# Dense inputs moved from the last chunk of z to the last chunk of turned sums in a DLRM tower, and an order laid out anew

## What is computed

```
e   = stack(tbl_f[ids[:, f]] for f in range(40))      # 2048 x 40 x 64
z_p = sum over d, c of e_i[d] * W_p[d, c] * e_j[c]    # 780 pairs
h   = concat([z, dense_ctx])                          # 780 + 16 = 796 inputs
h   = relu(h @ W_top1 + b_top1)                       # 796 -> 512
h   = relu(h @ W_top2 + b_top2)                       # 512 -> 256
y   = h @ W_top3                                      # 256 -> 1
```

## Time and profile before

| | us |
|---|---|
| median of 3 runs | 1236.45 (1236.43 to 1236.52) |
| the profiled execution | 1235.92 |
| its span, first to last instruction | 1234.1 |
| PE busy | 1216.8 (99%) |
| DVE busy | 1004.4 (81%) |
| ACT busy | 954.5 (77%) |
| POOL busy | 781.1 (63%) |

### The profile page before, as it was taken

The page is one execution under the profiler, slowest core; times in us unless marked ns, Lnnn a source line. Parts: engine busy times, 40 slices in busy tenths (PEclk is TensorE's granted clock), DMA queues, the critical chain, the costliest instruction groups (busy, mean ns, idle before and its releaser), DMA issues.

```text
span 1234.1 us, 23139 instructions
## 1 busy us (share of the span) xinstructions
PE 1216.8 (99%) x5912; PEld 445.5 (36%) x5912; DVE 1004.4 (81%) x916; ACT 954.5 (77%) x7377; POOL 781.1 (63%) x1038
## 2 busy tenths in 40 slices
PE   7999999999999999999999999999999999999999
PEld 3333333333333333333333333333333333333333
DVE  7898999998787788898767868889787876788850
ACT  2174878998383889999688899999778899999841
POOL 8888883686655577777656666778766566423320
DMA  7332222222222222222222222222222222111100
GB/s 200 110 86 66 67 75 58 70 70 65 64 64 60 50 76 64 65 75 63 70 58 59 68 57 66 67 74 65 61 71 65 62 59 61 54 49 57 43 10 1
DMA packets 68477, 81.00 MB, mean 66 GB/s; under 512 B 15308, under 2 KB 46028, under 8 KB 68216
## 3 DMA queue, kind: packets, MB, share of 16 engines
q1 hardware_dynamic: 48752, 59.42, 16.1%
q0 software_dynamic: 19456, 19.96, 9.0%
q10 hardware_dynamic: 136, 0.14, 0.0%
HBM read 79.45 MB, written 0.01 MB: 64 GB/s over the span
## 4 chain that ended last, share of the span: by engine, by line
PE 95%; DVE 3%; issue 1%; ACT 1%; DMA 0%; SPq 0%; DVEq 0%
PE u_ps L940 35%; PE u_ps L936 23%; PE z_ps L957 19%; PE turn_ps L988 7%; PE turn_ps L908 3%; PE turn_ps L901 2%; PE turn_ps L998 2%; PE u_ps L988 2%; DVE acts L1051 1%; DVE fprod L1088 1%; PE u_ps L998 1%; PE turn_ps L974 1%; DVE rprod_A L1075 0%; DMA rows<-in_first_ids 0%; PE turn_ps L1007 0%
## 5 line engine op out<-in xcount | busy, mean ns | idle before, releaser
L1145 ACT ACTIVATE rprod_A<-rprod_A 128x64 f32<-128x64 f32 x3616 | 866.3, 242 | 105.2 <-DVE rprod_A L1075 102.7
L845 POOL DMA_INDIRECT rows<-in_tbl,ids_all x608 | 575.3, 946 | 274.1 <-issue 112.6
L1145 ACT ACTIVATION_READ_ACCUMULATOR rprod_A<-rprod_A 128x1 f32 x3616 | 680.3, 188 | 0.0
L1088 DVE TENSOR_TENSOR fprod<-u_ps,x 128x1024 f32<-128x1024 f32 x480 | 567.4, 1219 | 50.6 <-PE u_ps L940 50.0
L940 PE MATMUL u_ps<-x,wf_ring 64*128 64x512 f32 x1920 | 490.1, 607 | 3.6 <-ACT x L1132 1.8
L1075 DVE TENSOR_TENSOR rprod_A<-u_ps,rows 128x1024 f32<-128x1024 f32 x226 | 274.9, 1222 | 131.5 <-PE u_ps L936 131.5
L936 PE MATMUL u_ps<-wr_ring,x 64*128 64x512 f32 x1280 | 347.5, 612 | 0.7 <-DVE rprod_A L1075 0.5
L940 PEld LDWEIGHTS u_ps<-x,wf_ring 64*128 64x128 f32 x1920 | 175.1, 186 | 252.9 <-issue 186.7
L957 PE MATMUL z_ps<-fprod,ones 128*32 128x512 f32 x1920 | 251.9, 598 | 0.0
L865 POOL TENSOR_TENSOR rprod_P<-rprod_P 128x512 f32<-128x512 f32 (+4 forms) x245 | 148.5, 606 | 131.3 <-DVE rprod_P L1075 115.4
L936 PEld LDWEIGHTS u_ps<-wr_ring,x 64*128 64x128 f32 x1280 | 116.7, 186 | 171.2 <-issue 93.7
(11 more groups left out here) (37 smaller groups left out, 193.2 us busy)
## 6 DMA issues: line engine op xcount, KB each, us to landing
wf_ring<-in_w_standing SPq DMA_DIRECT2D x240, 128.0 KB
wr_ring<-in_w_moving SPq DMA_DIRECT2D x80, 256.0 KB
rows<-in_tbl,ids_all POOLq DMA_INDIRECT x608
mlp_sb<-in_mlp SPq DMA_DIRECT2D x1, 2308.0 KB, 9.6
mlp_sb<-in_tbl SPq DMA_DIRECT2D x6, 224.0 KB
rows<-in_first_ids SPq DMA_DIRECT2D x4, 256.0 KB, 5.8
rprod_P<-in_first_ids SPq DMA_DIRECT2D x4, 256.0 KB, 8.8
mlp_sb<-in_tbl SPq DMA_DIRECT2D x2, 280.0 KB
```

The costliest lines, as they stand in the source:

```text
L845: nc.gpsimd.indirect_dma_start(rows[:, v % ROW_SLOTS, s, par * DIM:(par + 1) * DIM], None, tables[f], bass.IndirectOffsetOnAxis(ap=ids_all ...
L1088: nc.vector.tensor_tensor(fprod[:, f % FPROD_SLOTS], u_ps[:, bank:bank + 2, :], other, ALU.mult).then_inc(prods_done, 1)
L1145: op = nc.scalar.activation(of[:, j, :], of[:, j, :], ACT.Copy, accum_out=sums_at(u, j, 1))
```

## The change

DENSE_CHUNK and DENSE_ROW become the last chunk of turned sums and row 64 there (they were chunk 3 of z, row 96). With this `z_strips` gives four strips for the last chunk of z as well, `move_z` copies 128 rows of it in place of 96, layer 1 reads 128 rows of chunk 3 in place of 112 and 80 rows of chunk 6 in place of 64, and the dense DMA goes to z_sb's slot for chunk 6. That slot is one for all blocks, while the four chunks of z go round six slots. `lay_mlp` lays out W_top1 to match, on the host. Of the plan, seven constants are changed; the order of all steps is computed from them.

```diff
-DENSE_CHUNK, DENSE_ROW = (ZF - 1, 96) if Z_LAST <= 48 else (ZK - 1, R_PAIRS % P)
-assert Z_LAST <= 48 or 0 < DENSE_ROW <= P - DENSE
+DENSE_CHUNK, DENSE_ROW = (ZK - 1, R_PAIRS % P) if 0 < R_PAIRS % P <= 64 else (ZF - 1, 96)
+assert DENSE_CHUNK >= ZF or Z_LAST <= 48
...
-T_HOT, T_BUILD, T_TABLE, T_TABLES = 0.423, 0.35, 6.0, 1.6
-
-LEAD, LEAST, ROWS_LEAD = 4, 1, 4
-
-STALL, GAP = 0.05, -0.3
-
-MLP_GAP, MLP_PACE = 6, 14
+T_HOT, T_BUILD, T_TABLE, T_TABLES = 0.423, 0.535, 8.5, 1.6
+
+LEAD, LEAST, ROWS_LEAD = 8, 1, 5
+
+STALL, GAP = 0.05, 0.2
+
+MLP_GAP, MLP_PACE = 2, 12
```

## The result

The change makes the kernel faster by 2.3%: 1208.57 us (1208.33 to 1208.88, 4 runs) against 1236.44 us, a ratio of 0.9775 with a 95% interval of 0.9758 to 0.9792. That is 27.9 us where 22.6 were forecast. A second group of runs gave 0.9778 [0.9761, 0.9794].

What follows compares the result with a forecast made beforehand. The prediction took PE (busy 99%) as the bound, with DVE setting the pace in block 0 from 120 to 275 us. It summed -19.7 (strips) - 4 (start) + 1.1 (ROWS_LEAD) = -22.6, giving 1213.8 us, range 1207 to 1221.5.

Steps and rivals of the forecast that it cites:

- The group of sums: Chunk 3's 24 groups on PE: four strips cut each from 2.70 to 1.86 us, 20.4 on PE, -19.7 at the end.
- The estimate from the speedups of 3.07 and 2.38: Chunk 3's groups on PE: 2.09 us each, 14.6 saved in all; as a rival 1218.9 us, 3%.
- 18 x 0.85 come through: Last groups of blocks 1 to 3, where DVE waits for PE: 15.3 us of the strips' saving reaches the end.
- fillers: LEAD 8 and MLP pacing move duos and MLP steps to other stalls: 0, bounds -4 to +4 us.
- The start term (-4): Start of block 0: quad 2's moving units near 109 us instead of 115.31, closing DVE idle time; bounds 0 and -6.3.
- the price of 1.1: Block 0: ROWS_LEAD 5 moves one unit's sum from POOL to DVE, +1.1 us; extremes +8 and -5.
- the term of 4.4: DVE's six gaps after block 0's last groups: saving cut to the gap, 0.56 + 0.47 + 4 x 0.85 us.
- a bound of 1.6 for heights in layer 1: Layer 1's heights of 80 and 128 rows put at 0; bound 32 instructions by 49 ns, either way.
- Block 0 didn't eat its share: Rival: the order gives nothing and saturated DVE in block 0 turns PE's saving into waiting; -15.3 alone, 1221.2 us, 20%.
- the filler wasn't used up: Rival: MLP_GAP 2 spends MLP steps early in blocks 1 to 3, up to 57 us lost; half gives 1242, 5%.
- the change did what it said: Denies the rival that four-strip groups still wait for their products and nothing is gained: 1236 us, 2%.
- the rival of a better gain: Start's hole closes fully (-6.3), fewer V sums in block 0 (-4), all 20.4 of the strips: 1205.8 us, 8%.

## Why the prediction held, and where it was short

**The group of sums.** Right in size and in count: 1.86 us forecast, 1.85 measured, in 23 of 24 groups. The estimate from the speedups of 3.07 and 2.38 in TensorE: Matmul & The Clock Gate of the Trainium skill ("Measured speedup vs the span model") would have given 2.09, and the trace decides against it here. The 3.07 stands there for four row tiles, and these strips are column tiles, so the two speedups weren't of one kind. The step that failed in a small way is "18 x 0.85 come through": the very last group waits for its products (0.05 gained), so it is 17.

**Blocks 1 to 3.** -16.6 us to the last unit, where 17 groups give 14.5. The other 2.1 are left for the order, whose fillers the prediction put at 0 within 4 either way; the dense inputs' new place costs nothing here, as the 9.84 us show. Which constant does it wasn't separated.

**Block 0.** -8.9 against -7.3. The reasoning was that DVE sets the pace there, so that the gain is the idle time of DVE that goes away. That held: its idle time from 48 us to 10 us into block 1 fell from 18.5 to 7.5 us, against which it works 2.1 us more there. The start term (-4) was right: from 48 to 120 us idle time fell by 3.7, and quad 2 began at the time worked out from the constants. The V sums went from 24 to 25 as taken, while POOL's went from 7 to 5 and ACT's from 49 to 50; the price of 1.1 wasn't measured by itself. What was mis-sized is the term of 4.4 for the gaps behind the last groups: I cut each by 0.85 at most, and their idle time fell by 7.3 (8.3 to 0.9). The new order has five of DVE's own sums behind these groups where the old has two, and a sum of 1.13 with 0.85 from the strips closes a gap of 1.69. The trace of the order alone, with three strips, has these five sums and still gaps of 0.47 to 0.56 behind four of them, so both parts are needed to close them.

**ROWS_LEAD** stood in the sum as a cost of 1.1, and GAP at 0. The runs showed ROWS_LEAD to be a condition: the start constants without it leave two sums behind the last groups, and make the kernel slower by 16 us on a slower chip. With it, and with GAP still as before, there are five. What the sum had wrong is thus the place of the V sums and not their number. I looked at each constant by itself and not at what the earlier clock lets the plan do elsewhere. As both were in the change, the time forecast came out too long by this and not too short.

**The tail.** 0 forecast, with a bound of 1.6 for heights in layer 1; -1.6 measured. Four layer 1 steps in a row take 6.01 us in place of 6.40, since there is no longer a chunk of 64 rows between those of 128. I had the rows of the three heights and dismissed them by their mean durations; what differs isn't the duration of a matmul but when the next may start. My second theory, written down before the experiments, that the same thing costs 5.2 us in blocks 0 to 2, fell: counted to the next step of 128 rows nothing is lost.

**The rivals.** Block 0 didn't eat its share, the filler wasn't used up (from 500 to 550 us DVE is busy for 46.7 of 50, with PE full), and the change did what it said. The result lies between the forecast and the rival of a better gain, 1205.8. The terms that were short are all short of a gain, so that no error hid another. How the 27.9 us divide between strips and order on the first chip is read from its traces; neither part was run there alone. On the two slower chips the same strips brought 8 to 10 us and the order cost 3 to 5, so the size of the gain is shown for the first chip alone.

## What to carry to other kernels

When PE packs matmuls into strips of its array, count the rounds: eight matmuls over three strips take three turns, over four they take two, and the weight loads in the trace show it. Time saved on the busiest engine counts only where the engine behind it has idle time, so read that engine's gaps next to each saved piece. To see what a step costs, count up to a point that both kernels reach with the same work done: a unit that starts 0.43 us earlier may have only one half of the array ahead. Constants of a planner are judged together and on more than one chip: correcting two of them alone undid, on one chip, all that the strips gained.

## What the runs showed of the hardware

A matmul over 64 rows runs beside one on the other 64 rows even when they belong to different steps: the unit behind layer 1 began at 626.07, 0.5 us before layer 1's last instruction at 626.59. The lead is gone at the next step of 128 rows, which starts 8.12 us behind the start of layer 1 with it and 8.22 without it, 0.10 of that being lost in front. Between chunks of 128 rows one of 64 costs 0.39 us (6.40 against 6.01 for a step of seven).

On two of three chips, engines stood still without a wait while POOL gathered by indirect DMA. Between an ACTIVATE and the read of its accumulator, where ACT can't be waiting for anything, and before ACTIVATEs with no wait, the four traces from the third chip add up to 39 to 53 us of idle time each. All of it lies within 1.5 us of a gather or its pause, which is 77% of the span, and none in the other 23%. From 200 to 300 us, where POOL gathers little, there is none. On the first chip it is at most 0.1 us in the whole kernel, beside the same gathers. So gathers alone don't do it, and what makes the chips differ stays open.
